# A Mamba scan of 2 x 512 columns, issued as one instruction or as two that are counted apart

## The reference

```python
def _mamba_mixer(h, in_proj_w, conv_w, conv_b, x_proj_w, dt_proj_w, dt_proj_b, A_log, D, out_proj_w):
    xz = h @ in_proj_w                                   # 256 -> 2 x 512 channels
    u, z = jnp.split(xz, 2, axis=-1)
    u = jax.nn.silu(_causal_depthwise_conv(u, conv_w, conv_b))
    xdbl = u @ x_proj_w
    dt_r = xdbl[..., :R]                                 # R = 64
    Bm = xdbl[..., R:R + N]                              # N = 16 states
    Cm = xdbl[..., R + N:]
    dt = jax.nn.softplus(dt_r @ dt_proj_w + dt_proj_b)
    A = -jnp.exp(A_log)

    def step(hst, inp):
        dt_t, B_t, C_t, u_t = inp
        dA = jnp.exp(dt_t[..., None] * A)
        dBu = dt_t[..., None] * B_t[:, None, :] * u_t[..., None]
        hst = dA * hst + dBu
        y = jnp.einsum('bdn,bn->bd', hst, C_t)
        return (hst, y)
    ...
    y = jnp.swapaxes(ys, 0, 1) + u * D
    y = y * jax.nn.silu(z)
    return y @ out_proj_w
```

## Time and profile before

| | |
|---|---|
| median of 3 runs | 3242.48 us (3233.87 to 3245.94) |
| the profiled execution, its time | 3240.23 us |
| its span | 3238.4 us |
| mean granted TensorE clock | 0.936 |
| PE busy | 2729.4 us (84%) |
| DVE busy | 2379.4 us (73%) |
| ACT busy | 1873.3 us (58%) |
| POOL busy | 1823.9 us (56%) |
| first scan starts, last scan starts | 918.1 us, 2949.8 us |

### The profile page before, as it was taken

How to read it: one execution, slowest core, us unless ns; L and a number is a source line. 1 busy time by engine, 2 the same in 40 slices (tenths; PEclk the granted TensorE clock), 3 DMA queues, 4 the chain that set the end, 5 groups by cost and what they waited for, 6 DMA issues and landing times. The chain is left out here.

```text
span 3238.4 us, 47779 instructions
## 1 busy us (share of the span) xinstructions
PE 2729.4 (84%) x17006; PEld 2195.6 (68%) x17006; DVE 2379.4 (73%) x2432; ACT 1873.3 (58%) x2523; POOL 1823.9 (56%) x1211
## 2 busy tenths in 40 slices
PE   6999984891388999989989999899899999985693
PEld 5888873660157777777777777777777777884462
DVE  6888862672159788787797887877878878795473
ACT  4556660550377667576576675766766757651351
POOL 1112211443058677687686775866767768675354
PEclk8999996895699999999999999999999999998897
DMA  1111116123012021120120111202202112023523
GB/s 52 52 58 58 58 40 151 60 69 112 20 66 72 14 66 47 40 73 21 60 79 14 66 40 41 79 14 66 72 15 73 34 46 72 14 66 66 130 74 98
DMA packets 135893, 190.19 MB, mean 59 GB/s; under 512 B 28612, under 2 KB 109380, under 8 KB 135684
## 3 DMA queue, kind: packets, MB, share of 16 engines
q1 hardware_dynamic: 128196, 166.87, 16.7%
q0 software_dynamic: 7488, 20.46, 2.4%
HBM read 145.31 MB, written 41.98 MB: 58 GB/s over the span
## 5 line engine op out<-in xcount | busy, mean ns | idle before, releaser
L1281 POOL TENSOR_TENSOR m_state<-m_state,m_c_all 128x1024 f32<-128x1024 f32 x512 | 1204.3, 2367 | 508.9 <-DVE m_state L1373 508.9
L1373 DVE TENSOR_TENSOR_SCAN m_state<-m_decay,m_ps_d 128x1024 f32<-128x1024 f32 x512 | 1162.0, 2278 | 262.1 <-PE m_ps_d L1661 127.4
L1439 ACT ACTIVATE m_decay<-m_dt,m_aneg 128x511 f32<-128x511 f32 x1024 | 662.9, 711 | 103.8 <-DVE m_state L1373 103.1
L1674 PE MATMUL m_ps_y<-m_ident,m_state 128*128 128x128 f32 x4096 | 546.6, 278 | 75.9 <-POOL m_state L1281 75.9
L1661 PEld LDWEIGHTS m_ps_d<-m_bdiag,m_duT 128*128 128x128 f32 x4096 | 500.2, 196 | 126.6 <-issue 79.8
L1661 PE MATMUL m_ps_d<-m_bdiag,m_duT 128*128 128x128 f32 x4096 | 516.1, 281 | 58.3 <-DVE m_state L1373 46.7
L1674 PEld LDWEIGHTS m_ps_y<-m_ident,m_state 128*128 128x128 f32 x4096 | 475.8, 144 | 83.0 <-POOL m_state L1281 83.0
L1350 DVE TENSOR_TENSOR m_duB<-m_duT,m_ps_i 128x1024 f32<-128x1024 f32 x256 | 306.0, 1195 | 0.0
L1659 PEld LDWEIGHTS m_ps_d<-m_ident,m_duB 128*128 128x128 f32 x2048 | 242.1, 145 | 78.1 <-issue 63.2
L1659 PE MATMUL m_ps_d<-m_ident,m_duB 128*128 128x128 f32 x2048 | 275.7, 279 | 12.9 <-DVE m_state L1373 11.2
L1575 PE MATMUL m_ps_f<-m_hT,m_win 128*128 128x512 f32 x512 | 247.5, 608 | 13.3 <-DVE m_dt L1317 7.8
(11 more groups left out here) (194 smaller groups left out, 4495.7 us busy)
## 6 DMA issues: line engine op xcount, KB each, us to landing
m_c_all<-m_c_rows SPq DMA_DIRECT2D x128, 512.0 KB, 4.4
out<-m_xw SPq DMA_DIRECT2D x32, 512.0 KB, 3.0
f_y_rows<-f_y_sb SPq DMA_DIRECT2D x46, 256.0 KB, 2.1
a_xin<-x SPq DMA_DIRECT2D x16, 512.0 KB, 4.6
a_xres<-x SPq DMA_DIRECT2D x16, 512.0 KB, 5.4
x<-a_xout SPq DMA_DIRECT2D x16, 512.0 KB, 3.3
f_w_1b<-w1b SPq DMA_DIRECT2D x4, 2048.0 KB, 21.0
m_xin<-x SPq DMA_DIRECT2D x16, 512.0 KB, 4.1
```

The source lines that it names most:

```text
L1281: nc.gpsimd.tensor_tensor(s, s, c_all[:, n, :, :], ALU.mult).then_inc(weighed, 1)
L1373: nc.vector.tensor_tensor_scan(state[:, r, :, :].rearrange("p n t -> p (n t)"), decay[:, r, :, :].rearrange("p n t -> p (n t)"), ps_d[i % ...
L1439: ins = nc.scalar.activation(decay[:, r, j, 1:S], dt_sb[:, c, 1:S], ACT.Exp, scale=aneg[:, c, n:n + 1])
L1674: ins = nc.tensor.matmul(ps_y[:, t, :], state[:, i % RING, j, t * P:(t + 1) * P], id_sb[:, :], start=(n == 0 and j == 0 and t == 0), stop= ...
```

## The change

Each scan of 1024 columns becomes two of 512, one for each j, and `decay_ready`, `drive_full` and `scanned` count halves: every wait on them has its value doubled. PE waits for a half of the scan before the four products that overwrite this half's bank, and adds one to `drive_full` behind each four. ACT adds one behind each exponential. POOL still waits for both halves and multiplies 1024 columns at once, and the order of all other work stays.

```diff
--- before.py
+++ after.py
@@ -1274,7 +1274,7 @@
                 for i in range(UN):
                     if st.has(0):
                         b, n = st.item(0), i % NP
-                        pool.wait_ge(scanned, UN * b + i + 1)
+                        pool.wait_ge(scanned, 2 * (UN * b + i + 1))
                         if i < NP:
                             pool.wait_ge(c_loaded[n], 16 * (b + 1))
                         s = state[:, i % RING, :, :]
@@ -1313,7 +1313,7 @@
                 n = CT * b + k
                 dve.wait_ge(sp_exp, n + 1)
                 if st.has(o - 1):
-                    dve.wait_ge(decay_ready, UN * b - UN + NP * (k + 1))
+                    dve.wait_ge(decay_ready, 2 * (UN * b - UN + NP * (k + 1)))
                 nc.vector.scalar_tensor_tensor(out=dt_sb[:, k, :], in0=f_bank("DT", k)[:, :], scalar=0.0,
                                                in1=sp_e[:, :], op0=ALU.max, op1=ALU.add).then_inc(dt_part, 1)
 
@@ -1346,7 +1346,7 @@
                 if i == 0:
                     dve.wait_ge(bt_put, b + 1)
                 if i >= 2 * SR or st.has(o - 1):
-                    dve.wait_ge(drive_full, UN * b + i - 2 * SR + 1)
+                    dve.wait_ge(drive_full, 2 * (UN * b + i - 2 * SR + 1))
                 nc.vector.tensor_tensor(duB[:, r, :, :, :], duT[:, c, :, :].unsqueeze(1).to_broadcast([P, 2, TT, P]),
                                         ps_bt[h][:, 2 * n:2 * n + 2, :].unsqueeze(3).to_broadcast([P, 2, TT, P]),
                                         ALU.mult).then_inc(scaled, 1)
@@ -1356,7 +1356,7 @@
                 h, b = st.half(o), st.item(o)
                 dve.wait_ge(bt_ready, b + 1)
                 if st.has(o - 1):
-                    dve.wait_ge(drive_full, UN * b - NP + n + 1)
+                    dve.wait_ge(drive_full, 2 * (UN * b - NP + n + 1))
                 nc.vector.tensor_tensor(bdiag[:, n // 2, :, :], ps_i[:, 0:P].unsqueeze(1).to_broadcast([P, 2 * TT, P]),
                                         bt[h][:, 2 * n:2 * n + 2, :].rearrange("p n t -> p (n t)").unsqueeze(2)
                                         .to_broadcast([P, 2 * TT, P]), ALU.mult).then_inc(b_ready, 1)
@@ -1366,14 +1366,13 @@
                     if st.has(0):
                         g = UN * st.item(0) + i
                         r = i % RING
-                        dve.wait_ge(decay_ready, g + 1)
-                        dve.wait_ge(drive_full, g + 1)
                         if i >= RING or st.has(-1):
                             dve.wait_ge(summed, g - RING + 1)
-                        nc.vector.tensor_tensor_scan(state[:, r, :, :].rearrange("p n t -> p (n t)"),
-                                                     decay[:, r, :, :].rearrange("p n t -> p (n t)"),
-                                                     ps_d[i % 2][:, :, :].rearrange("p n t -> p (n t)"), 0.0,
-                                                     ALU.mult, ALU.add).then_inc(scanned, 1)
+                        for j in range(2):
+                            dve.wait_ge(decay_ready, 2 * g + j + 1)
+                            dve.wait_ge(drive_full, 2 * g + j + 1)
+                            nc.vector.tensor_tensor_scan(state[:, r, j, :], decay[:, r, j, :], ps_d[i % 2][:, j, :], 0.0,
+                                                         ALU.mult, ALU.add).then_inc(scanned, 1)
                     if i % 2 and i + 3 < UN and st.has(0):
                         scale(st, 0, i + 3)
                     if i % 2 and i + 3 >= UN and st.has(1):
@@ -1433,12 +1432,11 @@
                 if i % NP == 0:
                     act.wait_ge(dt_ready, CT * b + c + 1)
                 if i >= RING or st.has(o - 1):
-                    act.wait_ge(scanned, UN * b + i - RING + 1)
+                    act.wait_ge(scanned, 2 * (UN * b + i - RING + 1))
                 for j in range(2):
                     n = 2 * (i % NP) + j
-                    ins = nc.scalar.activation(decay[:, r, j, 1:S], dt_sb[:, c, 1:S], ACT.Exp,
-                                               scale=aneg[:, c, n:n + 1])
-                ins.then_inc(decay_ready, 1)
+                    nc.scalar.activation(decay[:, r, j, 1:S], dt_sb[:, c, 1:S], ACT.Exp,
+                                         scale=aneg[:, c, n:n + 1]).then_inc(decay_ready, 1)
 
             def softplus(st, o, k):
 
@@ -1463,7 +1461,7 @@
                 b = st.item(o)
                 act.wait_ge(du_full, CT * b + c + 1)
                 if st.has(o - 1):
-                    act.wait_ge(drive_full, UN * b - UN + NP * (c + 1))
+                    act.wait_ge(drive_full, 2 * (UN * b - UN + NP * (c + 1)))
                 nc.scalar.activation(duT[:, c, :, :].rearrange("p t d -> p (t d)"), f_bank("DU", c)[:, :],
                                      ACT.Copy).then_inc(duT_ready, 1)
 
@@ -1650,9 +1648,9 @@
                     pe.wait_ge(scaled, UN // 2 * b + i // 2 + 1)
                 elif c == 0:
                     pe.wait_ge(b_ready, NP // 2 * b + n // 2 + 1)
-                if i >= 2 or st.has(o - 1):
-                    pe.wait_ge(scanned, UN * b + i - 1)
                 for j in range(2):
+                    if i >= 2 or st.has(o - 1):
+                        pe.wait_ge(scanned, 2 * (UN * b + i - 2) + j + 1)
                     for t in range(TT):
                         drive_t = ps_d[i % 2][:, j, t * P:(t + 1) * P]
                         if n % 2 == 0:
@@ -1660,7 +1658,7 @@
                         else:
                             ins = nc.tensor.matmul(drive_t, duT[:, c, t, :], bdiag[:, n // 2, TT * j + t, :],
                                                    start=True, stop=True)
-                ins.then_inc(drive_full, 1)
+                    ins.then_inc(drive_full, 1)
 
             def add_up(st, o, i):
 
```

## The result

The changed kernel took 3259.11 us, the median of 6 runs (3256.24 to 3259.84), where the kernel before took 3244.06 us on the same chip, also 6 runs (3233.87 to 3247.54). The ratio is 1.0048, with a 95% interval of 1.0034 to 1.0062: slower by some 15 us, right at the bound of what the prediction called no change (0.5%), at the far end of its range (3227 to 3259), and 19 us above the time it named. The profiled execution took 3259.50 us, 19.3 us more than that of before.

The account below looks back on a forecast made before the run. A ring through PE, DVE, POOL and ACT bounds each item, DVE the last. Sum 9(12d - 0.60) + 5(7d - 1.47) + 32d = 175d - 12.75, -2.3 us at d = 0.06: 3240 us predicted, range 3227 to 3259.

Parts of the forecast that it names:

- The ring of four links: Path of one item passing between PE, DVE, POOL and ACT; an ordinary item was to change by 12d - 0.60 us.
- d: Extra DVE time per scan when two instructions of 512 columns replace one of 1024, taken as 0.06 us.
- Rival A: DVE's halves are dear: 175 extra starts on the path; at d = 0.19, 3263 us by the median; chance 0.12.
- The estimate of 0.125: About 125 ns for each DVE instruction on PSUM; as d it would make the sum about +9 us.
- Step 3: PE's third dt projection, ACT's exponentials, scan 26: its first half starts behind the first exponential, gain 0.60 us.
- Rival C: Halves hand nothing over, exponentials or drive halves being met at once; only 175d stays, 3253 us; chance 0.08.
- Step 2: Scans 13 to 15 on DVE, then POOL to unit 16: cost 3d, and PE's 3.68 us wait for POOL remains.
- if the POOL waits moved: Sign of being wrong: PE's 3.68 us waits for POOL, ahead of unit 16, should all still be there.
- 3d: Cost of the three split scans 13, 14 and 15 on DVE ahead of POOL, at d = 0.06 us each.
- rival B: PE carries step 4 everywhere and its clock gains: together -24 us, 3219 us by the median; chance 0.10.
- Step 4: DVE's scans from 26 to PE's U projection: cost 9d ordinarily; at a back edge 4d, with 0.87 us gained.
- 7d - 1.47: Change of each of five items at a back edge: seven extra starts less gains of 0.60 and 0.87 us.

Follow-up runs that it names:

- E1: Kernel before, only each scan split into two instructions of 512 columns, waits ahead and one count behind both, no half handed over: 3253.16 us, ratio 1.0036.
- E4: Changed kernel, but PE waits for both halves of the scan ahead of the first product: 3241.36 us, ratio 1.0000.
- E8: E3 with the loop written out, so no back edge: 3189.65 us, ratio 0.9841.
- E11: Kernel before, with three needless small multiplications on POOL at the end of `norm`, making POOL 0.46 us later: 3257.14 us, ratio 1.0038.
- E3: Changed kernel, with statistics on DVE moved from step 14 to 10 and `norm` on POOL from 15 to 11: 3195.56 us, ratio 0.9852.
- E7: E3, but PE waits for both halves of the scan before the first product: 3195.22 us, ratio 0.9853.
- E5: Changed kernel plus 24 needless transposes on PE at step 18, ahead of the add_up that waits for POOL: 3229.42 us, ratio 0.9958.
- E9: E5 with 4 transposes in place of 24: 3243.62 us, ratio 1.0002.
- E10: E5 with 12 transposes in place of 24: 3252.09 us, ratio 1.0029.
- E6: Kernel before, whole scans, plus the same 24 needless transposes on PE: 3222.52 us, ratio 0.9938.

## Why the prediction missed

- **What bounds the kernel: right.** The ring of four links was there after the change too, and each link named in the sum moved by what was said of it to 0.05 us.
- **The price of a second instruction: right.** d was taken as 0.06 and is 0.045 to 0.05 (two scans start to start, and nine scans in +0.41). Rival A needed 0.165 and is out; that the time fell near its 3263 says nothing for it. The estimate of 0.125 from the Trainium skill (Perfetto Trace Analysis, "Optimizing Scalar/DVE Operations") is not borne out either: this case measures 0.05, with one of the scan's inputs in PSUM. The prediction gave the Trainium skill, VectorE: DVE Perf Modes, "The DRAIN you can't avoid", only in part: the page says there too that a next operation that is not held starts earlier. The scans' starts 0.10 us ahead of the end fit that.
- **Step 3, the exponentials: right,** 0.62 us for the 0.60 forecast. Rival C is out by that, and by the waits at drive(31) (2.05 to 0.50) and ahead of the U projection (0.26 to 1.12).
- **Step 2, "POOL's 3.68 us remain": the step that failed.** The wait was read as a delay that the halves leave alone; the prediction named it as a sign of being wrong "if the POOL waits moved". It grew to 4.06 us, since PE's half lets it finish its drives sooner. The 3d of the scans ahead of POOL did not lengthen it: E1 and E4 have them too, and wait 3.62 and 3.63 us. The 0.15 us of path was in the sum. What was not is that PE comes out of the wait at 1.2 GHz, and does so more often and for longer: +13.6 us in 13 items. The prediction had read the clock behind the gap at drive(31) and let it speak for a gain alone (rival B). It counted 8 slow ones of 14; there are nine, and the one shown took 3.30 - 2.05 = 1.25 us more, not 1.35. There the gap shrank and the slow stretches did vanish, nine of them from 1162 to 2722 us, but in ordinary items they had cost nothing: with one at 1292 us the item is 129.18 us, and without one, in the changed kernel behind a short stretch, 129.18 as well (1125.57 to 1254.75). The place where the clock costs is where drive(18) is already late for DVE, and the prediction did not ask what the change does to that gap. The Trainium skill, Perfetto Trace Analysis, "Optimizing Scalar/DVE Operations", says that breaking up instructions may allow work to be completed sooner where Scalar or Vector cause bubbles on other engines. It did: PE was at this wait 0.43 us sooner (4.06 against E4's 3.63), and E4 shows that to be the harm.
- **Step 4 at the back edge: wrong.** The term 7d - 1.47 was to give -5.8 us with the d that was measured; the edges gave +3.6. PE came to the edge sooner, as said, but did not leave it sooner. In three cases it starts drive(1) 5.1 to 5.3 us after its last unmet wait (1428.78 to 1434.09 and 1691.64 to 1696.81 after, 1946.67 to 1951.81 before), in a fourth 5.5 us (1954.44 to 1959.94 after). So an earlier arrival became idle time, and the longer idle times went with a slow drive(1). E8 shows that the gap goes with the loop. PE's early start is not what makes the edges dear: in E4 and E11, without it, all five are slow as well. What inside the edge takes the time, and what sets the clock there, stays open.

Shown by experiment: 18 us of the changed kernel's time are PE's early start (E4), it needs the wait for POOL to do harm (E3, E7), filling that wait gives the loss back and more (E5, E9), and lengthening it without any halves costs some 11 us of clock beside the 6 of the delay itself (E11). Not shown by experiment, only counted from the traces: how the 19.3 us divide into 13.6 behind the waits and 3.6 at the edges. Open: what decides between none, short and long. It is not the wait's length alone: 3.6 to 3.7 us gave 14 none of 42 in before, E4 and E9 but 0 of 14 in E1, 2.74 us gave 4 of 14 (E10), and 4.13 us fewer long ones than 4.06 us (E11). Only the 0.8 to 1.9 us left in E5 and E6 gave none each time.

## What to carry over

Before an engine is allowed to start something earlier, ask where it will wait next: if the next wait is set by another engine, earliness only lengthens it, and on TensorE a longer standstill can be paid for again in the clock of the work behind it. Read the granted clock behind each of PE's waits, and count it as a cost only where the work behind the wait is already late for another engine. Where the wait can be removed (here, by moving `norm` and its statistics four steps up), do that first: the same split of scans that lost 15 us then gained 8, and with the loop written out the kernel runs in 3189.65 us, 1.6% under the one before.

## What the runs showed of the hardware

- Needless matmuls in a standstill of TensorE made the kernel faster: 24 transposes, 2.78 us, at 15 places (14 of them standstills) gave 30 us (E5) or 20 us (E6), and 4 of them, 0.44 us, gave 15.5 (E9). Twelve gave only 7, since the slow stretches at the back edges grew (E10).
- The stretches at 1.2 GHz at PE's waits came in lengths of 3.4 and 6.8 us, and 10.2 once; the long ones began while PE still stood still.
- A scan of 512 columns in f32 takes 1203 ns and follows the one before it after about 1.1 us, so that two cost only 0.045 to 0.05 us more than one of 1024, with two more waits and one more count between them.
- A back edge of the loop held PE for 1.7 to 4.0 us before and after the change, and for up to 4.83 in E5; written out, the same place has 0.80 us (E8).
